# Three of four accumulators are copied into place by ScalarE, and the extra one-hots multiply the weighted rows themselves

## What is computed

```
h = (x @ W).reshape(n_nodes, Hh, Cc)
a_src = (h * att_src).sum(-1)
a_dst = (h * att_dst).sum(-1)
alpha = leaky_relu(a_src[src] + a_dst[dst])
m = jax.ops.segment_max(alpha, dst, num_segments=n_nodes)
e = jnp.exp(alpha - m[dst])
denom = jax.ops.segment_sum(e, dst, num_segments=n_nodes)
w = e / jnp.clip(denom, 1e-16)[dst]
out = jax.ops.segment_sum(w[:, :, None] * h[src], dst, num_segments=n_nodes)
```

## Time and profile before

| | us |
|---|---|
| median of 3 runs | 6509.73 (6506.02 to 6517.36) |
| span of the profiled execution | 6515.9 |
| TensorE busy | 4981.0 (76%) |
| VectorE busy | 5313.4 (82%) |
| ScalarE busy | 2717.7 (42%) |
| GpSimd busy | 4585.1 (70%) |

### The profile page before, as it was taken

One profiled execution on the slowest core, in us unless ns is written; L12 is line 12 of the kernel. 1 busy time (PEld: TensorE's weight loads), 2 busy tenths in 40 slices (PEclk: granted clock), 3 DMA queues, 4 the chain that ended last, 5 costly groups with the idle time before them and its releaser, 6 DMA issues. The chain is left out here.

```text
span 6515.9 us, 110173 instructions
## 1 busy us (share of the span) xinstructions
PE 4981.0 (76%) x21652; PEld 3682.0 (57%) x21653; DVE 5313.4 (82%) x16735; ACT 2717.7 (42%) x4351; POOL 4585.1 (70%) x4837
## 2 busy tenths in 40 slices
PE   6788888888888577777777777758778778787876
PEld 5555655555556355555555555536656556566653
DVE  6788888888888788888888888877778778777788
ACT  3333333333333245554545455533333333333335
POOL 2777777777776577776767676737777777777764
PEclk8777877877777678777777777767777777778786
DMA  8555555555555455555555555535555555555545
GB/s 274 149 156 156 157 157 155 157 156 156 156 155 141 117 162 160 160 159 156 159 158 162 153 162 157 162 102 161 160 158 161 160 159 161 160 160 160 160 131 159
DMA packets 505894, 1027.11 MB, mean 158 GB/s; under 512 B 146891, under 2 KB 313199, under 8 KB 504878
## 3 DMA queue, kind: packets, MB, share of 16 engines
q0 software_dynamic: 226208, 633.50, 36.2%
q1 hardware_dynamic: 278798, 382.44, 18.1%
HBM read 931.37 MB, written 84.15 MB: 156 GB/s over the span
## 5 line engine op out<-in xcount | busy, mean ns | idle before, releaser
L1032 POOL DMA_INDIRECT e_rows<-table,loaded x4689 | 4489.2, 957 | 1756.8 <-issue 1392.6
L1266 PE MATMUL e_p_mm<-e_rows,e_onehot 128*128 128x264 f32 x9378 | 2466.5, 417 | 0.0
L1266 PEld LDWEIGHTS e_p_mm<-e_rows,e_onehot 128*128 128x128 f32 x9378 | 1876.3, 208 | 360.5 <-issue 20.1
L1444 DVE TENSOR_TENSOR e_rows<-e_rows,e_p_pair 128x1024 f32<-128x1024 f32 x1173 | 1417.8, 1209 | 0.0
L1436 DVE TENSOR_TENSOR e_onehot<-e_col,e_p_pair 128x512 f32<-128x512 f32 (+1 forms) x1467 | 953.4, 650 | 328.2 <-issue 280.4
L1259 PE MATMUL e_p_mm<-e_xmsg,e_onehot 128*128 128x264 f32 x1764 | 875.3, 669 | 103.3 <-ACT e_p_mm L1133 86.2
L1274 PE MATMUL e_p_one<-ad_parts,e_onehotT 128*128 x5586 | 707.8, 188 | 149.6 <-issue 143.3
L1225 ACT ACTIVATE e_rows<-e_gap 128x64 f32<-128x64 f32 (+1 forms) x294 | 80.6, 274 | 1621.0 <-DVE e_gap L1766 1614.7
L1274 PEld LDWEIGHTS e_p_one<-ad_parts,e_onehotT 128*128 128x128 bf16 x5586 | 550.4, 102 | 330.4 <-issue 193.3
L1139 ACT ACTIVATE e_onehotT<-e_onehotT,minus_pidx 128x2432 bf16<-128x2432 bf16 x294 | 681.0, 2316 | 42.0 <-DMA e_pass<-pass_rows 42.0
L1142 ACT ACTIVATE e_onehotT<-e_onehotT,one_col 128x2432 bf16<-128x2432 bf16 x294 | 682.6, 2322 | 9.6
(11 more groups left out here) (326 smaller groups left out, 5819.3 us busy)
## 6 DMA issues: line engine op xcount, KB each, us to landing
e_onehotT<-rel_rows SPq DMA_DIRECT2D x294, 608.0 KB
e_rows<-table,loaded POOLq DMA_INDIRECT x4689
e_own_row<-table SPq DMA_DIRECT2D x196, 128.0 KB
table<-e_rows_out SPq DMA_DIRECT2D x98, 132.0 KB
table<-n_rows_out SPq DMA_DIRECT2D x14, 910.0 KB, 15.6
table<-e_rows_out SPq DMA_DIRECT2D x98, 130.0 KB
n_inputs<-in_x_turned SPq DMA_DIRECT2D x14, 896.0 KB, 11.2
e_mask<-mask_rows SPq DMA_DIRECT2D x196, 64.0 KB
```

The lines of the kernel that those rows point to most:

```text
L1032: pool.indirect_dma_start(rows[k][:, g, 0:TW], None, table[L], bass.IndirectOffsetOnAxis(ap=idx[k][:, g:g + 1], axis=0)).then_inc(s_gat[k] ...
L1266: ins = nc.tensor.matmul(p_mm[:, bass.ds(region, MW)], onehot[:, g, :], rows[k][:, g, :], start=False, stop=True, skip_group_check=True)
L1444: return nc.vector.tensor_tensor(feats, feats, p_e[:, gs, :].unsqueeze(3).to_broadcast([P, n, H, C]), ALU.mult)
```

## The change

- `acc` has three more places at its end. Banks 1 to 3 of `p_mm` no longer begin at zero: ScalarE fills them with what already stands at the window's second to fourth place (`prepare_sums`, in the place of `clear_sums`), TensorE accumulates on top, and ScalarE copies them back (`spread`) before the next lookups. VectorE adds the first bank alone (`add_first`).
- The extras' one-hots multiply the gathered rows, weighted in place by the message step, and no longer a copy weighted apart: `xmsg` and VectorE's six steps for it are gone. Their three one-hots are made with the fourth quarter's. TensorE's extras move from ahead of the tops' transpose to between the factor's matmul and the fourth quarter's products.
- Because the extras now read `rows`, GpSimd waits for the extras of three windows back ahead of a window's first gather.
- The two logits are one tile, and one step takes the slope of both; a step that clamped the gap at zero is gone.
- VectorE loads its register words once a window; ScalarE and TensorE each load some that they did not.

```diff
+                    wait_apart(pool, st["extras"], ago(BUFS))
                     for g in range(tiles_of(w)):
                         if g % 4 == 0:
                             wait_apart(pool, s_mm[g // 4], ago(BUFS))
...
-                def clear_sums(done):
+                banks = p_mm[:].rearrange("p (r n) -> p r n", n=BANK)
...
+                def spread(off, done):
+
+                    act.wait_ge(s_mm[3], done)
+                    nc.scalar.copy(later_places(off), banks[:, 1:REGIONS, 0:MW]).then_inc(st["spread"], 1)
+
+                def prepare_sums(off, done):
 
                     act.wait_ge(s_ones, done)
-                    nc.scalar.copy(p_mm[:].rearrange("p (r n) -> p r n", n=BANK)[:, :, 0:MW],
-                                   zero_col.unsqueeze(2).to_broadcast([P, REGIONS, MW])).then_inc(st["cleared"], 1)
+                    nc.scalar.copy(banks[:, 0, 0:MW], zero_col.to_broadcast([P, MW]))
+                    nc.scalar.copy(banks[:, 1:REGIONS, 0:MW], later_places(off)).then_inc(st["cleared"], 1)
...
+                    if not first:
+                        older, old = words(act, WINDOW_ROW, w * WIN + W_BACK, 2, (PLACES - 1) * ACC_W)
+                        if not (isinstance(w, int) and w == 1):
+                            spread(older, ago(2))
...
-                    for e in range(EXTRAS):
+                def extras(k, slots, done):
+
+                    pe.wait_ge(st["msg3"], done)
+                    flat_rows = rows[k][:].rearrange("p g m -> p (g m)")
+                    for e, slot in enumerate(slots):
                         r = (1 + e) * BANK
-                        nc.tensor.matmul(p_mm[:, r:r + MW], onehot[:, G + e, :], xmsg[:, e, :], start=False, stop=True,
-                                         skip_group_check=True)
+                        last = nc.tensor.matmul(p_mm[:, r:r + MW], onehot[:, G + e, :], flat_rows[:, bass.ds(slot * MW, MW)],
+                                                start=False, stop=True, skip_group_check=True)
+                    last.then_inc(st["extras"], 1)
...
                     if not first:
-                        extras(past)
+                        wait_apart(pe, st["cleared"], past)
...
+                    if not first:
+                        extras((k - 1) % BUFS, old_slots, past)
                     products(3)
...
-                    for r, off in enumerate(offs):
-                        sums = acc[:, bass.ds(off, MW)]
-                        last = nc.vector.tensor_tensor(sums, sums, p_mm[:, r * BANK:r * BANK + MW], ALU.add)
-                    last.then_inc(st["added"], 1)
+                    sums = acc[:, bass.ds(off, MW)]
+                    nc.vector.tensor_tensor(sums, sums, p_mm[:, 0:MW], ALU.add).then_inc(st["added"], 1)
...
-                    ins = one_hot(4 * q, n, k, 4 * q, p_iota)
+                    ins = one_hot(4 * q, n + EXTRAS if q == 3 else n, k, 4 * q, p_iota)
...
-                    dve.wait_ge(st["dist"], now)
-                    nc.vector.tensor_scalar(gap[:], gap[:], 0.0, None, ALU.min).then_inc(st["gap"], 1)
```

More of the change, by code:

```diff
@@ L49 @@
 LONG = (WINDOWS - 1) * G + ROWS
[L50 removed]
+WINDOW_ENDS = 6
 BEGIN_AT = TILES
@@ L62 @@
 REGIONS = 4
+SPREAD = REGIONS - 1
 BANK = 512
@@ L929, in edge_phase @@
                 lin = sbuf(ph, tag + "lin", [P, 2, D], F32)
-            adst, l1, l2, gap = (sbuf(ph, tag + n, [P, G, H], F32) for n in ("adst", "l1", "l2", "gap"))
+            adst, gap = (sbuf(ph, tag + n, [P, G, H], F32) for n in ("adst", "gap"))
+            logit = sbuf(ph, tag + "logit", [P, 2, G, H], F32)
+            l1, l2 = logit[:, 0, :, :], logit[:, 1, :, :]
             fy, fl, fd, fdiff = (sbuf(ph, tag + n, [1, H], F32) for n in ("fy", "fl", "fd", "fdiff"))
@@ L1450, in far_blocks @@
                     if older is not None:
-                        wait_apart(dve, st["extras"], done)
+                        wait_apart(dve, st["expo"], done)
                     with dve.If(flag != 0):
@@ L1485, in far_blocks @@
                             dve.sem_inc(s_ones, 1)
-                def extras(k, slots, done, before):
-                    wait(dve, s_mm[0], before)
-                    dve.wait_ge(st["expo"], done)
-                    one_hot(G, EXTRAS, k, G, p_iota)
-                    if TOPS:
-                        dve.wait_ge(st["topread"], done)
-                    flat_rows = rows[k][:].rearrange("p g m -> p (g m)")
-                    for e, slot in enumerate(slots):
-                        feats = flat_rows[:, bass.ds(slot * MW, D)].rearrange("p (h c) -> p h c", h=H)
-                        weight = p_e_flat[:, bass.ds(slot * H, H)].unsqueeze(2).to_broadcast([P, H, C])
-                        nc.vector.tensor_tensor(xmsg[:, e, 0:D].rearrange("p (h c) -> p h c", h=H), feats, weight, ALU.mult)
-                        last = nc.vector.tensor_copy(xmsg[:, e, D:MW], flat_rows[:, bass.ds(slot * MW + D, MW - D)])
-                    last.then_inc(st["extras"], 1)
                 def quarter(k, q, done, before, n=4):
                     wait(dve, s_mm[q], before)
-                    ins = one_hot(4 * q, n, k, 4 * q, p_iota)
+                    ins = one_hot(4 * q, n + EXTRAS if q == 3 else n, k, 4 * q, p_iota)
                     if 4 * q + n in (G, LAST_TILES):
@@ L1674, in body @@
                     second = isinstance(w, int) and w == 1
-                    if not first:
-                        off, = words(dve, WINDOW_ROW, (w - 1) * WIN, 1, (PLACES - 1) * ACC_W)
-                        if not second:
-                            offs = words(dve, WINDOW_ROW, (w - 2) * WIN, REGIONS, (PLACES - 1) * ACC_W)
-                    flag, = words(dve, WINDOW_ROW, w * WIN + W_FLAG, 1, 2)
+                    older, old, flag = words(dve, WINDOW_ROW, w * WIN + W_BACK, 3, (PLACES - 1) * ACC_W)
                     m = mask[two]
@@ L1775, in body @@
                         carried(w, u, i)
-                    extras(k, slots, now, past)
                 nc.vector.memset(inb[:], -BIG)
@@ L1835, in _ @@
                 else:
-                    adds(offs, done)
+                    add_first(old, done)
                     merge(done)
```

107 lines of the change are left out of this document (59 added, 48 removed).

## The result

The changed kernel takes **6752.24 us** (median of 4 runs, 6740.05 to 6754.03) against 6508.19 us before on the same chip: a ratio of **1.0366, interval 1.0354 to 1.0378**, so it is slower by 244 us. The forecast was 6660 in a range of 6480 to 6820. The profiled execution of after has a span of 6750.3 us, 234.4 more than that of before.

What follows compares the result with a forecast made beforehand. GpSimd's gathers were taken to bound layers 0 and 2, VectorE layer 1. Layer terms +91, 0, +65 and ends -8 give +150 us on 6515.9, 6666; less 6 for the median, 6660 us, range 6480 to 6820.

Steps and rivals of the forecast that it cites:

- What bounds before: GpSimd's gathers set layers 0 and 2; VectorE savings can be worth at most layer 1's excess, 116 us.
- (a) VectorE's saving: VectorE drops three of four adds, some 1.0 us a window, plus extras' steps; busy time falls by some 800 us.
- (b) ScalarE: ScalarE's load and copy-out take 1.4 us; banks filled at +6.6 us after the scan, before TensorE needs them: hidden.
- rival 3: ScalarE also late if copy-out starts later than about +1.3: 6775 us, up to 6900; chance 0.15.
- (c) TensorE's clock: TensorE's products start 1.6 us earlier but run longer at the low clock, so the factor's matmul stays at +16.3.
- (d) the new wait and the ring: GpSimd's gathers wait for extras, start +19.0 not +17.2; scan-extras-gathers-scan chain spans two windows, layer 0 +91 us, layer 2 +65.
- The sign that it named: GpSimd's waits for TensorE grow from 157 us to several hundred, named by the extras' line, one per window.
- The loop's turn: Loop turning every six windows, now partly covered, could add 0 to 0.3 us a window, up to 85 us.
- The ends of the layers: The three ends of a layer save some 3 us each, -8 us together.
- Rival 1: GpSimd keeps its pace if extras are done by +16.4; layer 1 gains 116 us: 6395 us; chance 0.15.

Runs made afterwards that it cites:

- the fourth experiment: Changed kernel, but VectorE adds all four accumulators again and ScalarE clears the banks with zeros: 6939.75 us, ratio 1.0647 to before.
- the first and the last three experiments: Changed kernel with extras ahead of third quarter: 6621.07 us, unrolled 6481.34; with early first products and factor and extras ahead of third quarter: 6480.07, unrolled 6417.07.
- the first four experiments: Changed kernel with extras ahead of third quarter 6621.07 us; all windows written out 6668.66; extras behind fourth quarter 6960.99; VectorE adding all four accumulators 6939.75.
- the batch in two without a loop: Changed kernel, windows written out, banks filled between lookups, two tiles' products ahead of tops' transpose, factor and extras ahead of third quarter: 6417.07 us.

## Why the prediction was right, and which term was too small

- **What bounds before**: right. GpSimd's pace sets layers 0 and 2; the two kernels that reach it in all layers have periods of 20.04 to 20.19 us. No saving on VectorE was worth more than layer 1's excess: that excess, 117 us, is what before gains without a loop, and nothing more; there it goes with VectorE's work unchanged, as idle time of the loop.
- **(a) VectorE's saving**: right. 769 us of work went (some 800 predicted) and turned up as waiting at the scan.
- **(b) ScalarE**: right. The copies take 0.82, 0.37 and 0.81 us; the banks are filled at 1117.01, +6.2 (+6.6 predicted), ahead of the tops' transpose at +7.8. That was predicted at +8.05, with an estimate of 0.25 us for the semaphore; 0.15 pass in the window shown. The copy-out starts at -0.2 there and never behind the scan in windows 20 to 91, far from rival 3's deciding point of +1.3, and waits for products 78.3 us in all. Rival 3 falls by this and by the fourth experiment. In layer 1 the transpose comes 0.37 us later than in layer 0 (0.45 predicted).
- **(c) TensorE's clock**: right in layers 0 and 1. The products stand at the low clock now and the factor stays where it was: +15.95 and +16.30 as means, +16.07 and +16.16 before. In layer 2 it comes at +16.25, as predicted, but its mean before was +16.91; the +16.3 that the prediction read there was that of one window in which it came early. The products' mean rises from 417 to 467 ns, while that of the extras falls from 669 to 404. The window shown has the two levels of the earlier trace rows like this (us, PE busy, granted clock, DMA share, GB/s):

```profile
1118.60:1122.70 4.10, 4.10 (x10) 0.50 0.75 248
1122.90:1125.50 2.60, 2.60 (x14) 1.00 0.55 138
```

The rise to the high level is not fixed. It comes between +10.8 and +15.0 in single windows (20 to 91 of each layer), and the factor with it between +15.2 and +17.5: 0.47 to 0.50 us later for each us, as half speed has it. That is the spread which the prediction took in with its 110 us either way.
- **(d) the new wait and the ring**: right in place and size. The extras end at +17.9, +18.2 and +18.2 (+18.2 predicted), 0.91 us pass to the gather (0.8), the gathers start at +18.9, +19.1 and +19.1 (+19.0, in layer 1 +19.4). The sign that it named is there only in part: GpSimd's line names TensorE for 213.0 us in 116 windows, and the rest of the new wait stands under "issue".
- **The loop's turn: the term that was too small.** The prediction took it as 0 and gave "0 to 0.3 us a window, up to 85" as an end of the range, because it was hidden before. It measures 0.30, 0.33 and 0.25 us a window, 84 us, the far end of that range. The 23.1 and 22.8 us from gather to scan that went into the sum were read in windows away from a turn; the means of windows 20 to 91 before were 24.3 and 23.8, with 25.1 to 26.4 in the two windows at a turn. There this was harmless, since GpSimd ran on at its own pace. With GpSimd waiting for TensorE in most windows, a late scan makes a late row of gathers. GpSimd's late second gather, some 35 us by the estimate above, is the other thing that the sum lacks; it is still in the time without a loop.
- **The ends of the layers**: wrong in sign, small. They were to save 8 us and cost 16. The kernel after without a loop has 15 there, so it is not the turn; which step it is stays open. Some 3 of the 5 us ahead of the first scan appear in before without a loop too (161.2 against 158.3), which has nothing of the change.

Put together on the span, as predicted and measured:

| term | predicted | after | after without a loop |
|---|---|---|---|
| layer 0 | +91 | +110 | +81 |
| layer 1 | 0 | +12 | -19 |
| layer 2 | +65 | +96 | +72 |
| outside the layers | -8 | +16 | +15 |
| span | +148 | +234 | +149 |

The terms add up to 148, which the prediction rounds to 150. Without the turn that would have been right to 1 or 2 us, but by luck, since two errors cancel: the layers are 22 us below it, the ends 23 above. The last 8 us of the 92 between forecast and result are bookkeeping: the profiled execution of before was 6 us above its median, that of after 2 us below.

Rival 1 had its deciding point right and its price wrong. Extras done by +16.4 let the gathers start at +17.0 to +17.6 on the mean, as the first and the last three experiments show, but the time stayed above 6395: with TensorE's chain shortened and the loop gone as well the changed kernel still takes 6417.07.

## What to carry to other kernels

A transfer into a buffer starts when the buffer's last reader is done: who gives a buffer a new reader moves that transfer, and should place the reader as early as its inputs allow before counting what is saved elsewhere. Where a chain closes through that transfer over two windows, every delay in it counts, those that were hidden until then too; so look through the trace for idle time put down to nothing, such as a loop's turn, before taking it as covered, and read a whole turn of the loop and not one window. And an engine with the highest busy share may not be the bound: here the cheapest gain, 1.8%, lay in writing out a loop, not in relieving VectorE.

## What was not expected of the hardware

- A turn of the loop costs microseconds on several engines: 5.04 us of idle time on VectorE in layer 1 of before and 3.94 on TensorE in after, both under "issue". Without the loop such gaps are gone: 0.14 us ahead of layer 1's scans, and from ScalarE's copy of the scores to TensorE's transpose 0.3 to 0.4 us in the windows that had 2.2 to 2.4. The written-out code costs nothing that shows: the page counts 394 packets (6.46 MB) for the instruction queue of after without a loop and 477 (7.82 MB) with it. The Trainium skill (Runtime: NRT & Kernel Launch, Instruction fetch mechanics) says that a taken branch out of the prefetched pages stalls the engine on a fetch; these rows agree, though no run here separates the fetch from other costs of a turn.
- From the end of a matmul to the gather that waits for it 0.90 to 0.91 us pass, in 65 to 100% of the windows of after and of the first four experiments (20 to 91 of each layer), and the profile often books that wait as "issue".
- GpSimd's second gather of every sixth window comes some 1.6 us late, with and without a loop, where GpSimd has waited ahead of the row. Before without a loop, where it runs on, has none of this, and the batch in two without a loop has 0.5 to 0.8 us on the mean in 26 of 48 such rows. No run here shows why.
